# Holding each row gather until the last but one has landed, in a graph layer with experts

## The reference

```python
x_rel = einsum('nd,rdo->rno', layernorm(x), w_full)      # w_full[r] = sum_b w_comp[r,b] * weight[b]
msg = x_rel[etypes, src] * norm                          # 200000 edges, sorted by dst
agg = segment_sum(msg, dst, num_segments=N)
x = x + relu(agg + h_bias + layernorm(x) @ loop_weight)
x = x + layernorm_of(top-2-of-16 expert FFN(layernorm(x)) + its input)
```

## Time and profile before

| | us |
|---|---|
| median of 3 runs | 3274.21 |
| lowest and highest run | 3268.51 and 3275.11 |
| span of the profiled execution | 3302.6 |
| of this, `graph_layer` from its first gather to its last, 197.9 to 2656.9 | 2459.0 |

### The profile page before, as it was taken

How to read it: one execution, slowest core, us unless ns; L and a number is a source line. 1 busy time by engine, 2 the same in 40 slices (tenths; PEclk the granted TensorE clock), 3 DMA queues, 4 the chain that set the end, 5 groups by cost and what they waited for, 6 DMA issues and landing times. The chain is left out here.

```text
span 3302.6 us, 40335 instructions
## 1 busy us (share of the span) xinstructions
PE 2355.1 (71%) x11549; PEld 1953.5 (59%) x11550; DVE 965.9 (29%) x2172; ACT 658.4 (20%) x1539; POOL 1809.3 (55%) x2000
## 2 busy tenths in 40 slices
PE   2579898877778766767757565654744547999987
PEld 1467777666667555545545454543533337999986
DVE  6352332332223211222122121211211235333338
ACT  3232322222112211101110100000000004333336
POOL 0536566566565665656656566566565612555544
PEclk9699999888889888888878777876876678999999
DMA  6243333333333333323333332222322245122236
GB/s 214 85 133 97 108 96 105 94 97 116 96 97 95 107 96 93 96 87 94 106 90 90 93 95 88 86 85 83 91 85 82 81 127 211 70 70 70 69 95 229
DMA packets 146266, 338.62 MB, mean 103 GB/s; under 512 B 36674, under 2 KB 56290, under 8 KB 146051
## 3 DMA queue, kind: packets, MB, share of 16 engines
q0 software_dynamic: 89296, 245.33, 24.9%
q1 hardware_dynamic: 39311, 59.54, 5.2%
q10 hardware_dynamic: 17588, 32.88, 3.0%
HBM read 292.84 MB, written 47.97 MB: 103 GB/s over the span
## 5 line engine op out<-in xcount | busy, mean ns | idle before, releaser
L1060 POOL DMA_INDIRECT rows<-feat,idx x1540 | 1463.5, 950 | 974.7 <-DMA rows<-feat,idx 552.8
L1271 PE MATMUL psW<-rows,S 128*128 x3920 | 1155.5, 462 | 675.5 <-SPq L1016 647.9
L1271 PEld LDWEIGHTS psW<-rows,S 128*128 128x128 f32 x3920 | 910.0, 237 | 916.7 <-issue 752.3
L1142 DVE TENSOR_TENSOR S<-psHere,coefS 128x896 f32<-128x896 f32 x280 | 302.0, 1090 | 1798.9 <-PE psW L1271 1334.8
L1330 ACT COPY z<-psW 128x512 f32<-128x512 f32 x196 | 114.6, 585 | 1820.1 <-PE psW L1271 1185.2
L1236 PE MATMUL psG<-wb,zT 128*128 128x256 f32 (+1 forms) x1600 | 353.9, 379 | 0.5 <-issue 0.5
L1236 PEld LDWEIGHTS psG<-wb,zT 128*128 128x128 f32 (+1 forms) x1600 | 300.4, 188 | 46.5 <-issue 1.2
L1721 PE MATMUL psH<-xT,w1x 128*128 128x128 f32 x1840 | 227.0, 277 | 0.2
L1721 PEld LDWEIGHTS psH<-xT,w1x 128*128 128x128 f32 x1840 | 216.6, 193 | 2.0 <-issue 1.9
L1730 PE MATMUL psO<-w2s,hT 128*128 x912 | 215.7, 379 | 0.0
L1672 POOL DMA_INDIRECT expert_rows<-os,at_rows x114 | 113.1, 992 | 172.6 <-DVE os L1779 172.6
(11 more groups left out here) (284 smaller groups left out, 1472.2 us busy)
## 6 DMA issues: line engine op xcount, KB each, us to landing
rows<-feat,idx POOLq DMA_INDIRECT x1568
g<-expert_rows SPq DMA_DIRECT2D x24, 512.0 KB, 5.5
w1s<-in_L_ffn_w SPq DMA_DIRECT2D x8, 1024.0 KB, 10.0
w2s<-in_L_ffn_w SPq DMA_DIRECT2D x16, 512.0 KB, 9.9
feat<-rows SPq DMA_DIRECT2D x24, 256.0 KB, 3.0
fts<-feat ACTq DMA_DIRECT2D x24, 256.0 KB
h<-in_x ACTq DMA_DIRECT2D x24, 256.0 KB
y_rows<-y ACTq DMA_DIRECT2D x24, 256.0 KB
```

What stands on the lines that cost most here:

```text
L1060: e.indirect_dma_start(rows[:, at * H:(at + 1) * H], None, d.feat, bass.IndirectOffsetOnAxis(ap=idx[:, q * GB + u:q * GB + u + 1], axis=0) ...
L1142: e.tensor_tensor(S[h0 + h][:, :].rearrange("p (s b n) -> p s b n", s=U, b=B), both[:, h * U:(h + 1) * U, :].unsqueeze(2).to_broadcast([P, ...
L1271: last = e.matmul(psW[:, bass.ds(bank[u], H)], S[h][:, u * ZC:(u + 1) * ZC], rows[:, bass.ds(slot[u], H)], start=False, stop=True, skip_gr ...
```

## The change

Each gather now has a semaphore of its own out of eight in rotation (block j uses j modulo 8), and each is issued only when the gather two before it has landed, in `ahead` as in `blocks`. SyncE waits for each block alone and adds 1 to `s_in`. Registers that carry a threshold are now passed through one register operation, the maximum with 1, into a register of their own, on every engine that waits for such a value: GpSimd 8 per 112 gathers, TensorE 2 per turn and 1 per tile, VectorE 1 per tile and 1 per weight copy in the experts, ScalarE 8 per tile. The diff, without those of ScalarE and VectorE:

```diff
-QB = 7
+ROWS = 8
+AHEAD = 2
...
+def at_least_one(e, loaded, held):
+
+    for to, of in zip(held, loaded):
+        e.reg_alu(to, of, 1, ALU.max)
+    return held
...
             def ahead(j):
-                e.indirect_dma_start(rows[:, j * H:(j + 1) * H], None, d.feat, bass.IndirectOffsetOnAxis(ap=idx[:, j:j + 1], axis=0)).then_inc(s_row[j // QB], 16)
+                if j >= AHEAD:
+                    e.wait_ge(s_row[(j - AHEAD) % ROWS], 16 * ((j - AHEAD) // ROWS + 1))
+                e.indirect_dma_start(rows[:, j * H:(j + 1) * H], None, d.feat, bass.IndirectOffsetOnAxis(ap=idx[:, j:j + 1], axis=0)).then_inc(s_row[j % ROWS], 16)
...
             def rows_in(i):
-                for q in range(RB // QB):
-                    e.wait_ge(s_row[q], 16 * QB * (i + 1))
-                    e.sem_inc(s_in, QB)
+                for j in range(RB):
+                    e.wait_ge(s_row[j % ROWS], i * (RB // ROWS * 16) + (j // ROWS + 1) * 16)
+                    e.sem_inc(s_in, 1)
...
-                e.wait_ge(s_row[n % RB // QB], i * (IB * GB // RB * 16 * QB) + (n // RB + 1) * 16 * QB)
+                e.wait_ge(s_row[n % ROWS], i * (IB * GB // ROWS * 16) + (n // ROWS + 1) * 16)
                 e.sem_inc(s_paced, 1)
 
             def blocks(i):
                 e.load(regs, room[0:1, bass.ds(i * IB, IB)])
-                free = [e.snap(r, min_val=1, max_val=TURNS) for r in regs]
+                free = at_least_one(e, regs, room_held)
...
                     for u in range(GB):
                         at = (q * GB + u) % RB
-                        if u % QB == 0:
-                            landed(i, q * GB + u - QB)
-                        e.indirect_dma_start(rows[:, at * H:(at + 1) * H], None, d.feat, bass.IndirectOffsetOnAxis(ap=idx[:, q * GB + u:q * GB + u + 1], axis=0)).then_inc(s_row[at // QB], 16)
+                        landed(i, q * GB + u - AHEAD)
+                        e.indirect_dma_start(rows[:, at * H:(at + 1) * H], None, d.feat, bass.IndirectOffsetOnAxis(ap=idx[:, q * GB + u:q * GB + u + 1], axis=0)).then_inc(s_row[at % ROWS], 16)
...
-                        tile1 = e.snap(regs[AT_TILE], min_val=1, max_val=NT2)
                         with e.If(e.snap(regs[AT_ENDED], min_val=0, max_val=1)):
-                            tile_product(tile1, TW)
-                        clear = e.snap(regs[AT_CLEAR], min_val=1, max_val=NWP // 2)
-                        come = e.snap(regs[AT_COME], min_val=1, max_val=NBLK)
+                            tile_product(e.snap(at_least_one(e, regs[AT_TILE:AT_TILE + 1], tile_held)[0], min_val=1, max_val=NT2), TW)
+                        clear, come = at_least_one(e, [regs[AT_CLEAR], regs[AT_COME]], held)
```

More of the change, by code:

```diff
@@ L84 @@
 CTL_PART = (84, 72, 64, 60)
-assert NBLK % RB == 0 and RB % GB == 0 and RB % QB == 0 and sum(CTL_PART) == TURNS and all(n % NS == 0 for n in CTL_PART)
+assert NBLK % RB == 0 and RB % GB == 0 and RB % ROWS == 0 and AHEAD < ROWS and sum(CTL_PART) == TURNS and all(n % NS == 0 for n in CTL_PART)
 assert all(t + n <= 8 * i <= TURNS for t, n, i in CHUNK)
@@ L1030, in _ @@
             ch = Chain(e, s_pool)
-            regs = [e.alloc_register(f"room{q}") for q in range(IB)]
+            regs, room_held = ([e.alloc_register(f"{n}{q}") for q in range(IB)] for n in ("room", "room_held"))
             last = NBLK // (IB * GB) - 1
@@ L1118, in nodes @@
                 last.then_inc(s_y, 1)
-            regs = [e.alloc_register(f"look{k}") for k in range(2)]
+            regs, look_held = [e.alloc_register(f"look{k}") for k in range(2)], [e.alloc_register("look_held")]
             def look(i):
                 e.load(regs, pairs[0:1, bass.ds(i, 1), :])
-                tile1 = e.snap(regs[1], min_val=1, max_val=NT2)
                 with e.If(e.snap(regs[0], min_val=0, max_val=1)):
-                    nodes(tile1, P)
+                    nodes(e.snap(at_least_one(e, regs[1:2], look_held)[0], min_val=1, max_val=NT2), P)
             def pair(i, t0, c0, h0):
@@ L1254, in _ @@
             regs = [e.alloc_register(f"ps{u}") for u in range(CTL)]
+            held, tile_held = [e.alloc_register(f"ps_held{k}") for k in range(2)], [e.alloc_register("tile_held")]
             for part_of, n_turns in enumerate(CTL_PART):
@@ L1315, in _ @@
                 e.dma_start(to[0:1, :], zero[0:1, :]).then_inc(s_st, 16)
-            regs = [e.alloc_register(f"end{k}") for k in range(TW // 2)]
+            regs, ends = ([e.alloc_register(f"{n}{k}") for k in range(TW // 2)] for n in ("end", "end_held"))
             def tiles(t, nw):
                 e.load(regs, wend[0:1, bass.ds(t * (TW // 2), TW // 2)])
+                end = at_least_one(e, regs, ends)
                 base, groups = t * NE, HC * nw // 4
@@ L1327, in tiles @@
                         features_in(t, nw * WIN // 2)
-                    e.wait_ge(s_P, regs[k])
+                    e.wait_ge(s_P, end[k])
                     bank = psW[:, k % NB * BANK:(k % NB + 1) * BANK]
@@ L1750, in _ @@
         def _(e):
-            regs = [e.alloc_register(f"gx{k}") for k in range(SB + 2)]
+            regs, part_held = [e.alloc_register(f"gx{k}") for k in range(SB + 2)], e.alloc_register("part_held")
             e.wait_ge(s_bt, 1)
@@ L1761, in copy_w1 @@
             def copy_w1(k, ex):
-                e.wait_ge(s_wx, e.snap(ex // EG + 1, min_val=1, max_val=len(s_win)))
+                e.reg_alu(part_held, ex // EG + 1, 1, ALU.max)
+                e.wait_ge(s_wx, part_held)
                 e.tensor_copy(w1x[k][:, :], w1s[:, bass.ds(ex, 1), :, :].rearrange("p e c f -> p (e c f)")).then_inc(s_w1, 1)
@@ L2026, in program @@
                   [sb(f"choice{k}", [P, NT, X]) for k in range(K)], sb("both", [P, X, NT], BF16))
-        sent, got, s_row, s_xin, s_out, s_win = sems("sorted", 2), sems("got", 8), sems("row", RB // QB), sems("x_in", XS), sems("x_out", 2), sems("w_in", 4)
+        sent, got, s_row, s_xin, s_out, s_win = sems("sorted", 2), sems("got", 8), sems("row", ROWS), sems("x_in", XS), sems("x_out", 2), sems("w_in", 4)
         with nc.sbuf_tensor("ident_i", [P, P], F32) as ident_i:
```

## The result

The changed kernel takes 3599.4 us in the median against 3272.5 us before, measured beside it: a ratio of 1.100, interval 1.099 to 1.102, or 327 us more. Forecast were 3563 us, 289 us above the median of before that was shown.

The account below looks back on a forecast made before the run. GpSimd's gathers in a row were taken to bound the graph layer: 1539 intervals at 1.777 us, +5 start, -4 end, 2736 us against 2459, so +277. On the median that gave 3551 to 3572; forecast 3563 us, range 3490 to 3650.

Parts of the forecast that it names:

- the long step: GpSimd in the graph layer: one gather's start through landing and restart to the next start, 3.52 us, paid once per two.
- the mean: Graph layer, 600 to 2600 us: start-landing-restart averages 3.554 us over 179 cases, so 1.777 us per gather.
- Start, the first eight gathers: Start of the graph layer: weights' loads share the DMA engines, GpSimd gets off four gathers, not seven: +5 us.
- Long restarts: Graph layer: 22 gaps of 2.19 us instead of 1.25, costing 21 us before, should vanish in the spare time.
- rival 4: Restart grows by serial instructions, or one chain's delays push the other: 0.10 us more per gather, 3717 us in all; 10%.
- The end: After the layer's last gather: two turns, 7.90 us, before; with single blocks all but the last are done, -4 us.
- The early gathers: Of 28 before the layer, the last fourteen pace at 1.76 us, ending 6.5 us later, covered by 34.10 idle: cost 0.
- The rest of the edit: Waits, increments, threshold operations and SyncE's single waits, on all engines: hidden behind longer waits, each taken at cost 0.
- The 28 us between span and median: Whole kernel: median 28.4 us below the profiled span, perhaps from recorded long gaps; 3563 us taken between 3551 and 3572.
- The sum over two starts: GpSimd's gathers in the changed profile: 3.5 us over two starts; forecast wrong if under 3.4 or above 3.7.
- Waits for landings: GpSimd in the graph layer: nearly every gather ends one, some 1530 in place of 219.
- GpSimd's wait for room at the gathers: Graph layer: 0.3 us before; the forecast is wrong if GpSimd waits for room.
- A landing that gets shorter with fewer in flight: Graph layer gathers: pair takes 2.92 us, 1.46 per gather, stage 212 us less, 3062 us in all; chance 4%.

Follow-up runs that it names:

- the repeated changed kernel: The changed kernel, unaltered, measured once more beside the kernel before with only the maximum operations, on the same chip: 3598.6 us, ratio 1.099.
- the register part: The kernel before with only the maximum operations on thresholds; holds and handing over in sevens stay: 3310.2 us against 3308.9, ratio 1.0007; 3275.8 us on the faster chip.
- the doubled increment: The changed kernel with the semaphore increment behind each hold doubled: 3730.2 us, on the slower kind of chip.

## Why the prediction was right, and where it was off

**The bound and the law were right.** GpSimd's gathers in a row set the stage; the pace with n in flight is the long step divided by n, until the issue gap of 1.25 us is longer. It held for one (3.557 us), two (1.818, of which 1.764 is the law's; the rest is in the sum below), and five (1.281, on the faster kind of chip). With three, on the slower kind, it did not set the time (1.78 to 1.84 us): TensorE did. The step itself was forecast at 3.52 to 3.55 us and is 3.53 in the median.

**The sum for the stage was 48 us too small.** The forecast of 277 us holds 4 us that are saved behind the last gather, so it is 281 for the stretch of the gathers; 329.5 were measured, on one chip. Its total of 2740 us for that stretch was 57 too low, and the old stretch is 9 us longer on this chip (2467.9) than in the profile that it started from. By its terms, from the starts of the 1540 gathers of the repeated changed kernel:
- 1539 intervals at the median pace of 1.7655 us: 2717. I had 2735 with the mean.
- Start, the first eight gathers: +5.5, forecast +5.
- *Long restarts:* +32. This is the term that failed. I had seen 2.19 us gaps in place of 1.25 and said that they would vanish in the spare time. I take them to be those of the earlier trace rows. The kernel before and the register part have 21 of them (the prediction counted 22), 70 gathers apart. In the changed kernel they are 106 apart, 14 of them, and each start comes 3.35 us after the landing that it waited for, in place of 0.77; in all three kernels the first is ahead of the gather with number 113 of the layer, counted from 0:

```profile
367.66 0.98 POOL L1069 DMA_INDIRECT rows<-feat,idx  x1 [0.94 <-DMA rows<-feat,idx]
371.70 0.95 POOL L1069 DMA_INDIRECT rows<-feat,idx  x1 [3.05 <-issue]
372.95 0.95 POOL L1069 DMA_INDIRECT rows<-feat,idx  x1 [0.31 <-issue]
375.29 0.94 POOL L1069 DMA_INDIRECT rows<-feat,idx  x1 [1.40 <-DMA rows<-feat,idx]
```

The gather at 371.70 has 3.05 us of gap and no releaser, and delays both chains, so the spare time of a pair doesn't hide it. With sevens held but single blocks handed over, those that show stand at the same gathers as in the changed kernel, so the spacing doesn't come from holding two. There the one ahead of gather 749 falls on a long step and makes it 6.18 us:

```profile
1387.08 0.95 POOL L1072 DMA_INDIRECT rows<-feat,idx  x1 [0.30 <-issue]
1393.26 0.94 POOL L1072 DMA_INDIRECT rows<-feat,idx  x1 [5.23 <-issue]
```

With five in flight the landing lies far enough back: the gathers at the same 14 places start 3.35 to 3.6 us after theirs, but together they lose only some 4 us. More instructions per gather don't bring them closer, as the doubled increment left the 106. What they are stays open.
- Edges of the loop of 112 gathers: +6. I had counted nothing.
- The rest, +37: delays from the tiles' traffic and one chain pushing the other. I had 18 for it, the part of the mean above the typical step. One in seven was exposed to such delays before and the others hid them; the mean over single long steps leaves out that two chains share one queue. This is my reading of the remainder; no run separates the two.

The sum is 2797. My low estimate comes from the last two and the long restarts together (6, 37 less the 18, and 32: 57 us); rival 4, a restart that grows by serial instructions, was not it, as the typical restart is unchanged. Its second half, one chain pushing the other, is in the 37 us, a quarter of what that rival put down.

**The end** shortened as forecast. In the changed kernel one turn stands behind the last gather, not two as in the earlier trace rows:

```profile
2960.95 0.95 POOL L1069 DMA_INDIRECT rows<-feat,idx  x1 [1.59 <-DMA rows<-feat,idx]
...
2965.10 5.69 PE L1278 MATMUL psW<-rows,S 128*128 x14 [5.16 <-SPq L1026]
2970.83 0.59 ACT L1338 COPY z<-psW 128x512 f32<-128x512 f32 x1 [124.16 <-PE psW L1278]
```

From the last gather's start to the last turn's end: 9.8 us, and 13.4 before.

**The early gathers** I put at 0: they were to end 6.5 us later, behind 34.10 us of idle time. On the faster kind of chip that idle time is only 15.26 us, and they end 15.0 us later: the last fourteen begin 2.5 us later and start 2.21 us apart in the mean, not 1.76. First the last one with the register part alone, then that of the changed kernel and what follows it:

```profile
141.01 0.95 POOL L719 DMA_INDIRECT rows<-feat,idx  x1 [0.30 <-issue]
```

```profile
155.99 0.94 POOL L722 DMA_INDIRECT rows<-feat,idx  x1 [0.36 <-DMA rows<-feat,idx]
161.13 0.15 POOL L1070 IOTA xno<- 128x16 f32 x1 [4.20 <-POOLq L656]
```

So the layer starts 4 us later.

**The rest of the edit** at 0 was right: registers 1.0007, and single blocks are a gain of 17 us on one kind of chip (3308.9 to 3291.7), where I had 4 at the end of the stage. Of the 17.6 us by which the spans of the two profiles differ (3307.0 and 3289.4), 1.4 lie ahead of the layer's gathers, 9.3 among them and 6.9 behind. Why, was not followed up.

**The 28 us between span and median** I read as perhaps the recording's, and moved the forecast up by 12 us for it. It was the chip: on the faster kind the register part's span is 3274.0 for a time of 3275.8 us. The move helped by luck.

**The signs.** The sum over two starts (3.53 us) and TensorE's wait (923 us, forecast 900) came as named. Waits for landings came at 822 gathers and not 1530, the long gaps did not vanish, and GpSimd's wait for room at the gathers, which was to be a sign against the forecast, came three times for 3.2 us in all (8.1 in the repeated run), too little to count.

**The rivals.** A landing that gets shorter with fewer in flight fell: 2.75 us with one, two or seven. By the page of the Trainium skill that I had weighed (DMA: Bandwidth & Descriptors, Anatomy of one DMA) it would be an estimated 2.30 us; no run shows that, the measurement decides. In the earlier trace rows the data end at 2.3 us, so that the 0.45 us to the last increment come on top.

## What to carry to other kernels

A hold on transfers has a price that can be read before it is built: the time from start through landing to the next start, divided by how many may be in flight, against the gap of issue. Here it takes three in flight to hide it (3.53 / 1.25 = 2.8; measured only with five allowed), and any rule that allows fewer, or drains the queue, pays; a group of seven that drains pays once in seven. Small periodic gaps on the bounding engine need not disappear in a new wait because there is spare time on average, and a profile is to be compared with one from the same chip.

The version with five in flight beats the kernel before by 15% where it ran, and so the changed kernel by more. Three in flight, which should come to nearly the same (starts 1.25 us apart and 2.75 to a landing leave at most three under way), are 8 to 11% slower than before on the other kind of chip. Five there, and three on the faster kind, were not run, so it is shown as a gain for one kind of chip only.

## What the runs showed that I had not expected

Two kinds of chip, 1% apart for the kernel before, react in opposite ways to more gathers in flight. TensorE reports finished work by incrementing a semaphore. I matched each matmul or transpose that does so with the next increment recorded for it, from 200 to 2650 us, and counted those over 0.8 us behind its end. On the faster kind: 0 of 563 (register part), 0 of 534 (changed kernel), 1 of 995 (five in flight). On the slower: 182 of 567 (register part), 181 of 566 (sevens, single blocks), 215 of 519, 212 of 527 and 208 of 524 (three in flight), but 52 of 519 with two in flight (doubled increment) and 2 of 345 with one. Records are missing here and there, so each count is good to about ten. So on that kind of chip TensorE's signals come late more often when more gathers are under way. Whether their number counts or their pace, no run separates: 1.6 us per gather in sevens, 1.88 with two, 3.56 with one. In the kernel before the late signals don't lengthen the main loop, since the gathers are slower still: the register part's stretch is 2460.9 us on the slower kind and 2467.9 on the faster, and its layer starts 39 us later. Why one kind does it and the other doesn't, no run tells. The changed kernel itself, with its hold of two, was only measured on the faster kind, where the signals aren't late. The nearest run on the slower kind is the doubled increment, 3730.2 us in one execution against 3308.9 before, so nothing suggests that a hold of two gains there.
